# Issuing the mix of a first-layer attention block in two halves, four steps apart

## The reference, cut to what matters

```python
scores = jnp.einsum('bhqd,bhkd->bhqk', q, k) / math.sqrt(D)
scores = jnp.where(mask, scores, neg_inf)
attention = jax.nn.softmax(scores, axis=-1)
out = jnp.einsum('bhqk,bhkd->bhqd', attention, v)
out = out.transpose(0, 2, 1, 3).reshape(Bt, St, E)
return out @ Wo.T + bo
```

## Time and profile before

| what | us |
|---|---|
| median of 3 runs | 275.84 |
| lowest and highest run | 275.27 and 276.56 |
| span of the profiled execution | 273.6 |
| TensorE busy | 252.8 |
| VectorE busy | 212.9 |
| ScalarE busy | 191.3 |
| GpSimd busy | 181.2 |

### The profile page before, as it was taken

The page is one execution under the profiler, slowest core; times in us unless marked ns, Lnnn a source line. Parts: engine busy times, 40 slices in busy tenths (PEclk is TensorE's granted clock), DMA queues, the critical chain, the costliest instruction groups (busy, mean ns, idle before and its releaser), DMA issues.

```text
span 273.6 us, 6702 instructions
## 1 busy us (share of the span) xinstructions
PE 252.8 (92%) x1903; PEld 200.2 (73%) x1903; DVE 212.9 (78%) x654; ACT 191.3 (70%) x454; POOL 181.2 (66%) x271
## 2 busy tenths in 40 slices
PE   7987998999788999999999999999989999979994
PEld 5555666666556777777777888777777778878993
DVE  3799898889978896979778777777798625985673
ACT  2578798889697886965777666677776664656462
POOL 7357999777679776646664475449757795936380
PEclk9999999999999999999999999999999999999999
DMA  6557565300005666534475667756542051211530
GB/s 194 193 169 219 223 229 134 103 2 4 1 9 115 146 140 135 129 84 106 99 216 149 175 173 186 190 126 174 129 127 60 11 149 38 85 34 39 185 112 19
DMA packets 25987, 32.91 MB, mean 120 GB/s; under 512 B 4000, under 2 KB 18144, under 8 KB 25824
## 3 DMA queue, kind: packets, MB, share of 16 engines
q1 hardware_dynamic: 25520, 32.27, 43.8%
q10 hardware_dynamic: 432, 0.22, 0.3%
HBM read 14.32 MB, written 3.47 MB: 65 GB/s over the span
## 4 chain that ended last, share of the span: by engine, by line
PE 67%; DVE 11%; issue 9%; POOL 9%; ACT 3%; DVEq 0%; POOLq 0%; ACTq 0%
PE bank L1229 16%; PE bank L1398 14%; PE bank L1360 5%; PE bank L1234 5%; PE bank L1236 5%; PE bank L1235 5%; PE bank L1361 5%; PE bank L1354 4%; POOL q L648 3%; DVE masked L943 2%; POOL probs L604 2%; PE bank L1421 2%; PE bank L1413 2%; PE bank L1478 1%; DVE probsT L960 1%
## 5 line engine op out<-in xcount | busy, mean ns | idle before, releaser
L604 POOL TENSOR_SCALAR probs<-probs,rsum 128x512 f32<-128x512 f32 x128 | 87.9, 693 | 57.4 <-DVE rsum L952 56.5
L747 ACT ACTIVATE probs<-masked,neg_max 128x512 f32<-128x512 f32 x128 | 91.9, 719 | 11.9 <-DVE neg_max L943 9.1
L1229 PE MATMUL bank<-ident,probs 128*128 128x128 f32 x512 | 77.9, 275 | 0.8 <-ACT probsT L756 0.8
L1229 PEld LDWEIGHTS bank<-ident,probs 128*128 128x128 f32 x512 | 60.0, 141 | 14.6 <-issue 8.2
L943 DVE CUSTOM_DVE_ANT_0 masked<-bank,mask 128x512 f32<-128x512 f32 x64 | 43.8, 684 | 15.3 <-PE bank L1361 14.8
L756 ACT ACTIVATE probsT<-bank 128x512 f32<-128x512 f32 x74 | 43.5, 588 | 16.2 <-PE bank L1229 15.9
L1398 PE MATMUL bank<-probsT,val 128*32 128x256 f32 (+1 forms) x512 | 46.6, 384 | 0.0
L960 DVE COPY probsT<-bank 128x512 f32<-128x512 f32 x54 | 36.7, 680 | 11.4 <-PE bank L1229 11.1
L943 DVE CUSTOM_DVE_ANT_0 masked<-bank,shared 128x512 f32<-128x512 f32 x64 | 43.3, 677 | 0.4 <-PE bank L1354 0.3
L1354 PE MATMUL bank<-parts 128*128 128x512 f32 x64 | 31.3, 490 | 8.9 <-DVE neg_max L943 8.7
L1398 PEld LDWEIGHTS bank<-probsT,val 128*32 128x32 f32 (+1 forms) x512 | 24.4, 123 | 17.7 <-issue 5.1
(11 more groups left out here) (238 smaller groups left out, 525.4 us busy)
## 6 DMA issues: line engine op xcount, KB each, us to landing
k_both<-k_low SPq DMA_DIRECT2D x32, 128.0 KB, 2.8
k_both<-k_high SPq DMA_DIRECT2D x32, 128.0 KB, 2.7
q<-q_split SPq DMA_DIRECT2D x32, 128.0 KB, 2.4
probsT<-staged_gate SPq DMA_DIRECT2D x32, 128.0 KB, 3.0
q<-q_split SPq DMA_DIRECT2D x32, 64.0 KB, 2.1
parts<-staged_k SPq DMA_DIRECT2D x7, 256.0 KB, 2.8
w_flat<-in_w SPq DMA_DIRECT2D x1, 1536.0 KB, 8.0
staged_k<-k_high SPq DMA_DIRECT2D x2, 512.0 KB, 3.1
```

What stands on the lines that cost most here:

```text
L604: pool.tensor_scalar(p, p, rsum[:, u % NCOL:u % NCOL + 1], 1.0, ALU.mult, ALU.mult).then_inc(normed, 1)
L747: act.activation(probs[:, u % NP, :], masked[:, u % NS, :], ACT.Exp, scale=-1.0, bias=neg_max[:, c:c + 1], accum_out=sums[:, c:c + 1]).the ...
L1229: ins = pe.transpose(dst[0:rows, t * P:t * P + P], src, ident[:, :])
```

## The change

A first-layer block's mix is issued in two calls: key chunks 0 and 1 at `mix_at`, chunks 2 and 3 four steps later. In the last block of a batch (`g` = 3) both stand at `mix_at`, one behind the other. `mixed` is raised by the call that has the last chunk. Each call repeats the mix's waits. Two entries of `VALUES_AT` move: the value copies for blocks 5 and 6 on GpSimd go from steps 22 and 29 to 26 and 35. The second layer's mixes are issued as before.

```diff
+        self.later_half = 4 if g < 3 else 0
...
-VALUES_AT = {4: (0, (0, 1, 2, 3)), 20: (1, (0,)), 22: (1, (1,)), 29: (1, (2,)), 37: (1, (3,))}
+VALUES_AT = {4: (0, (0, 1, 2, 3)), 20: (1, (0,)), 26: (1, (1,)), 35: (1, (2,)), 37: (1, (3,))}
...
-            def mix(k):
+            def mix(k, parts):
...
-                for i in range(NK):
+                for i in parts:
                     for h in range(k.heads):
                         ins = pe.matmul(mix_bank[w * h:w * h + w, 0:SQ], v[:, i, w * h:w * h + w],
                                         probsT[:, k.m % 2, h, i, :], start=(first and i == 0), stop=(last and i == NK - 1))
-                ins.then_inc(mixed, 1)
+                if NK - 1 in parts:
+                    ins.then_inc(mixed, 1)
...
-                    if t == k.mix_at:
-                        mix(k)
+                    if k.layer == 0:
+                        for half in range(2):
+                            if t == k.mix_at + half * k.later_half:
+                                mix(k, (2 * half, 2 * half + 1))
+                    elif t == k.mix_at:
+                        mix(k, range(NK))
```

## The result

The changed kernel took **273.52 us** (median of 4 executions, 273.24 to 273.69) against 275.55 for the kernel before (4 executions, 274.55 to 276.56). The ratio is 0.9932, with a 95% interval of 0.9908 to 0.9955: faster by 0.7%. The forecast was 273.6. It started from the 275.84 of the first three executions of the kernel before; started from 275.55, the same sum would have given 273.36.

A forecast was written before the change was run, and what follows sets the result against it. TensorE and VectorE were taken to be late in turn in the first layer. Block savings 0.40 + 0.79 + 0.79 + 0 + 0.36 - 0.15 = 2.19 us, from 275.84, gave 273.6 us; range 272.4 to 275.1.

The forecast's parts named there:

- What bounds the kernel: First layer, 20 to 110 us: VectorE waits 7.4 us for TensorE's transposes, TensorE 7.5 us for VectorE's row maximum, by turns.
- The price of a visit: Split mixes on TensorE: a half takes 0.93 us, and each extra visit costs 0.09 + 0.06 = 0.15 us at its ends.
- one rival: Extra visits cost more than 0.15 us: chance 0.06 for slower, 0.07 for 0.3 to 0.6 each (274.4 to 275.9 us).
- 2.92 - 5c: Total saving in us over the split blocks, with c the cost of an extra visit; zero at c = 0.58.
- Blocks 1 and 2: First-layer mixes: first half saves 0.93 us, second half adds 0.14 of VectorE wait; 0.79 us saved in each block.
- Block 0: First mix: TensorE's idle time of 0.55 us limits the gain; less one extra visit, 0.40 us saved.
- The rival that GpSimd sets the pace: GpSimd bounds units up to 30, so blocks 0 and 1 save nothing lasting: 1.00 us saved, 274.8 us; chance 0.14.
- Block 4: Mix before the feed-forward's quantising: both halves covered while TensorE waits for VectorE; 0 us, bounds -0.2 and +0.2.
- Block 5: First half gains 0.93 us; second half's 1.08 less 0.51 of TensorE idle time hands on 0.57; 0.36 us saved.
- more comes out: Modelled idle figures too small: blocks 0 and 5 may give their full 0.93, 4.2 us saved, 271.6 us; chance 0.07.
- Block 6: TensorE is the bound by then and the extra visit costs 0.15 us: -0.15 us, bounds -0.3 and +0.3.
- The sum and the carry: All blocks together save 2.19 us, and whatever is gained before 87 us is carried to the end.

## Why the prediction was right, point by point

- **What bounds the kernel.** Right. The two waits of the earlier trace rows are taken apart by the change, block by block, and each block works by itself (0.84 and 0.85 in the run with blocks 1 and 2 alone). The waits for transposes fell to 4.2 us where about 3.5 was forecast, and 2.7 of them (1.03 and 1.68) sit at blocks 3 and 7, as forecast. The new waits at units 22 and 30 are 0.21 and 0.16, below the 0.3 that was named as a sign of dear visits.
- **The price of a visit: the mis-sized term.** The half was put at 1.87 / 2 = 0.93 and an extra visit at 0.15, from its two ends. But 0.13 of the 1.87 belongs to the visit and not to the records, as the pieces of 8, 16 and 32 records show. A half is 1.00, it spares 0.87 (the 0.86 at unit 17), and an extra visit costs 0.13 + 0.15 = 0.28. That is just below the 0.3 to 0.6 that one rival named. The prediction had said itself that no row of before shows a visit as short as 16 records; halving the 1.87 took it as all records. By the prediction's own formula, 2.92 - 5c, a c of 0.28 gives 1.52 saved and 274.3 us, inside its range; that 2.00 came out is due to blocks 0, 5 and 6, below.
- **Blocks 1 and 2.** Forecast 0.79 each, measured 0.55 and 0.58. The step "0.93 + 0.15 = 1.08 against 0.94 spare" with the true prices is 1.00 + 0.15 = 1.15, a loss of 0.21, and the first half is 0.87: 0.66. Measured losses are 0.27 to 0.32. Some 0.1 remains; the copy's wait of 0.16 is seen, the rest is not settled.
- **Block 0.** Forecast 0.40, measured 0.48, but for another reason. The forecast held that TensorE's own work takes the rest; it is GpSimd. With the clears elsewhere block 0 keeps 0.83 to 0.85, so the limit of 0.55 from TensorE's idle figures did not exist. The rival that GpSimd sets the pace was right in kind, but at block 0, at the transposes of unit 12, and not around unit 30 where the prediction looked for it; it costs 0.35 and not 1.19.
- **Block 4.** 0 forecast within 0.2 either way, -0.15 measured; whole, it is 0.
- **Block 5.** 0.36 forecast, 0.66 measured (1.46 to 2.12): a first half of 1.01, which holds a little of what block 4's second half had cost (with block 4 whole it is 0.86), and a loss of 0.35 against 0.57. The second half did push the copies back, but less than its 1.15 against the idle figure of 0.51 would have it (0.64); the prediction's rival "more comes out" named this weakness of modelled ends. What gave the additional room was not traced.
- **Block 6.** -0.15 forecast, -0.12 measured, and leaving it whole loses nothing. The number is met by luck: at 0.28 a visit the same reasoning gives -0.28, and TensorE was not simply the bound there, since the first half wins 0.83 before the second gives back 0.95.
- **The sum and the carry.** 2.19 forecast, 2.00 measured at unit 72 and 1.98 at unit 112: what is gained before 87 us is carried. The errors (-0.45 in blocks 1 and 2 together, +0.08 in block 0, +0.30 in block 5, -0.15 in block 4, +0.03 in block 6) partly cancelled; the time was met more closely than its terms.
- **0.22 lost between units 116 and 120.** Not foreseen. It also appears in the run where only value copies moved and the ruler shows no gain, so it is not a price of the halves. VectorE's routing steps and GpSimd's steps beside them, before:

```profile
201.41 0.47 DVE L1120 TENSOR_TENSOR_SCAN small<-ones,small 128x32 f32<-128x32 f32 x2
201.92 0.27 DVE L1122 TENSOR_TENSOR small<-small,room 128x64 f32<-128x64 f32 x1
202.22 0.79 DVE L1123 TENSOR_TENSOR small<-small 128x64 f32<-128x64 f32 x1
```

```profile
201.66 0.45 POOL L610 TENSOR_SCALAR w_early<-we 128x256 fp32r<-128x256 f32 x1
202.20 0.73 POOL L612 TENSOR_TENSOR w_early<-we,w_early 128x256 fp32r<-128x256 f32 x1
```

and in the changed kernel:

```profile
199.15 0.74 DVE L1121 TENSOR_TENSOR_SCAN small<-ones,small 128x32 f32<-128x32 f32 x2
199.92 0.79 DVE L1123 TENSOR_TENSOR small<-small,room 128x64 f32<-128x64 f32 x1
200.74 0.22 DVE L1124 TENSOR_TENSOR small<-small 128x64 f32<-128x64 f32 x1
```

```profile
199.41 0.41 POOL L611 TENSOR_SCALAR w_early<-we 128x256 fp32r<-128x256 f32 x1
199.90 0.73 POOL L613 TENSOR_TENSOR w_early<-we,w_early 128x256 fp32r<-128x256 f32 x1
```

Which VectorE step meets which GpSimd step differs: before, one step stretches from about 0.22 to 0.79; after, that stretch falls on the step ahead of it, and the scan is 0.27 longer beside GpSimd's first step. This is read from the rows; no run put the two out of each other's way.

## What to carry to other kernels

A lump in one engine's queue that starves another can be cut, and a cut is worth the wait it takes off, less what the later piece, the fixed price of its visit included, exceeds the consumer's spare time: put the later piece where the consumer has had time to build up spare, and leave whole the lumps behind which nobody waits, or behind which the wait only moves to the second piece (block 6). Take the fixed part of a visit from pieces of two sizes, since half of a whole hides it. When a wait shrinks, look at every other engine's queue at the same place, fillers such as clears above all, and put these where their engine idles and no chain on VectorE runs beside it.

## What the runs showed of the hardware

- **Some VectorE steps stand while GpSimd works.** The quantising step L1050 took 1.07 us instead of 0.39 beside a clear of 0.74 us, and ended 0.14 and 0.15 us behind GpSimd's instruction in the two traces. The Trainium skill, "SBUF — State Buffer", section "SBUF: two separate sides", says that the port pair which VectorE and GpSimd share is an exclusive lock held for a whole instruction; these traces agree. Not every step stands: the mask behind it, which reads the score bank, took its 0.68 us beside a GpSimd step of 1.03 us in both.
- **A gap on TensorE can cost time behind it as well, by the granted clock.** After 2.08 us of waiting in the quantising stretch the granted clock fell to between 0.50 and 0.61 in both kernels with the clears at 40 and 42, whose executions all had a mean clock below 1.00. The changed kernel, with a wait of 1.31 there, stayed at 1.00 in its trace. The run with two steps waited 1.30 and fell to 0.50 all the same, and a mix of 16 records took 1.87 us there instead of 1.00. What set it apart was not settled: TensorE was busy 2.06 of the 4 us before the fall, and in the changed kernel 2.07 of 4 us (66 to 70) without one. A low mean alone does not say that time was lost: one execution of the changed kernel had 0.992 and took 273.48.
- **A mix of 8, 16 or 32 records took 0.57, 1.00 and 1.87 us**, a fixed 0.13 beside 0.054 per record, and 0.15 more at its two ends among full-width matmuls. The Trainium skill, "TensorEngine Tiling (Array Packing)", section Key Properties, has the drain at a change of tiling mode that speaks against such cuts; the runs give the whole visit a price of 0.28 us, without telling how much of it is the drain.
